# Quantised expert in finer steps: some of VectorE's work on GpSimd and ScalarE, transposes in place of products with ones

## What is computed

```python
x = _layernorm(x + attention(x))        # linear attention, 16 heads, chunks of 128, decay, rotary, RMS norm
x = _layernorm(x + expert(x, fside, ctx))   # one expert per batch entry
x = _layernorm(x + ffn(x))              # fp4 weights, silu gate, I = 1408, RMS of the output

def _smooth_quant_linear(x, w):
    s = max(sqrt(max(amax_x, EPS) / max(amax_w, EPS)), EPS)   # maxima over rows, one per column
    xs, ws = x / s, w * s
    x_scale = max(rowmax|xs|, EPS) / 127;  w_scale = max(rowmax|ws|, EPS) / 127
    x_q = clip(round(xs / x_scale), -127, 127);  w_q = clip(round(ws / w_scale), -127, 127)
    return x_q @ w_q.T * x_scale * w_scale.T

def _expert_forward(xe, guw, dw):       # guw 512x512, dw 512x256, both differ per batch entry
    gate, up = split(_smooth_quant_linear(xe, guw))
    return _smooth_quant_linear(silu(gate) * up, dw)
```

## Time and profile before

| | |
|---|---|
| median of 3 runs | 863.43 us (862.97 to 863.92) |
| the profiled execution, its time | 862.34 us |
| its span | 860.5 us |
| PE, DVE, ACT, POOL busy | 87%, 63%, 37%, 15% |
| mean granted TensorE clock | 0.936 |

### The profile page before, as it was taken

One profiled execution on the slowest core, in us unless ns is written; L12 is line 12 of the kernel. 1 busy time (PEld: TensorE's weight loads), 2 busy tenths in 40 slices (PEclk: granted clock), 3 DMA queues, 4 the chain that ended last, 5 costly groups with the idle time before them and its releaser, 6 DMA issues.

```text
span 860.5 us, 12175 instructions
## 1 busy us (share of the span) xinstructions
PE 749.3 (87%) x4742; PEld 612.8 (71%) x4742; DVE 544.0 (63%) x1032; ACT 321.1 (37%) x559; POOL 129.4 (15%) x173
## 2 busy tenths in 40 slices
PE   4799988887998799525999999999999999899993
PEld 3688777766877587414888777886768877688882
DVE  3567578775667758769771847855578746542214
ACT  4232232225422432157443335353443544341312
POOL 0452334023322233044000000000000000000000
PEclk9899999997998899655999999999999999999997
DMA  8400100013100130040102012002111030010201
GB/s 306 171 26 1 38 13 13 1 26 123 32 7 1 38 99 1 1 147 1 50 1 74 0 50 98 1 25 98 48 53 45 0 122 1 1 50 0 98 1 49
DMA packets 25356, 41.11 MB, mean 48 GB/s; under 512 B 4954, under 2 KB 7642, under 8 KB 25178
## 3 DMA queue, kind: packets, MB, share of 16 engines
q1 hardware_dynamic: 23194, 37.27, 12.9%
q10 hardware_dynamic: 2112, 3.15, 1.1%
HBM read 28.88 MB, written 11.53 MB: 47 GB/s over the span
## 4 chain that ended last, share of the span: by engine, by line
PE 39%; DVE 8%; ACT 2%; issue 2%; DVEq 0%; ACTq 0%
PE ps L1460 24%; PE ps L1470 11%; PE ps L457 2%; DVE act_s L279 2%; PE ps L468 2%; DVE act_s L376 1%; DVE silu L1393 1%; ACT silu L1330 1%; PE ps L477 1%; DVE xc L1406 1%; ACT h_hi L1313 1%; DVE xb L406 1%; DVE e_stats L409 1%; PE ps L450 1%; DVE w L279 0%
## 5 line engine op out<-in xcount | busy, mean ns | idle before, releaser
L1460 PE MATMUL ps<-x2T_lo,wgu_hi 128*128 128x512 f32 x352 | 141.1, 401 | 0.8 <-DVE x2T_lo L1383 0.8
L1460 PE MATMUL ps<-x2T_hi,wgu_lo 128*128 128x512 f32 x352 | 137.3, 390 | 0.0
L1460 PE MATMUL ps<-x2T_hi,wgu_hi 128*128 128x512 f32 x352 | 137.2, 390 | 0.0
L1393 DVE TENSOR_TENSOR silu<-ps,silu 128x512 f32<-128x512 f32 x44 | 30.4, 690 | 100.2 <-PE ps L1460 99.9
L1045 PE MATMUL ps<-wqkv_lo,xT_hi 128*128 128x512 f32 x192 | 83.0, 433 | 10.5 <-DVE masked L972 6.2
L1045 PE MATMUL ps<-wqkv_hi,xT_lo 128*128 128x512 f32 x192 | 78.4, 408 | 0.0
L1045 PE MATMUL ps<-wqkv_hi,xT_hi 128*128 128x512 f32 x192 | 78.2, 407 | 0.0
L1460 PEld LDWEIGHTS ps<-x2T_lo,wgu_hi 128*128 128x128 f32 x352 | 66.2, 188 | 15.3 <-DVE x2T_lo L1383 1.5
L1460 PEld LDWEIGHTS ps<-x2T_hi,wgu_lo 128*128 128x128 f32 x352 | 66.1, 188 | 14.0
L1460 PEld LDWEIGHTS ps<-x2T_hi,wgu_hi 128*128 128x128 f32 x352 | 66.2, 188 | 12.9
L1470 PE MATMUL ps<-wdn_lo,h_hi 128*128 128x512 f32 x176 | 70.6, 401 | 3.7 <-DVE h_lo L1377 3.7
(11 more groups left out here) (170 smaller groups left out, 1473.8 us busy)
## 6 DMA issues: line engine op xcount, KB each, us to landing
x_in<-in_x_dram SPq DMA_DIRECT2D x16, 256.0 KB, 3.5
w<-in_fside_BxS2xS_dram SPq DMA_DIRECT2D x4, 1024.0 KB, 6.5
x_dram<-xb SPq DMA_DIRECT2D x4, 1024.0 KB, 5.1
xc<-x_dram SPq DMA_DIRECT2D x4, 1024.0 KB, 5.4
xb<-x_dram SPq DMA_DIRECT2D x3, 1024.0 KB, 5.4
out_dram<-xc SPq DMA_DIRECT2D x3, 1024.0 KB, 4.2
z<-in_x_dram SPq DMA_DIRECT2D x3, 768.0 KB, 4.7
x_dram<-z SPq DMA_DIRECT2D x3, 768.0 KB, 4.0
```

The lines of the kernel that those rows point to most:

```text
L1393: nc.vector.tensor_tensor(silu[:, it % 2, :], ps[5][:, :], silu[:, it % 2, :], ALU.mult)\
L1460: last = nc.tensor.matmul(dst[:, :], lhs, rhs, start=(k == 0 and n == 0), stop=(k == NK - 1 and n == 2))
```

## The change

What it does:
- The expert's steps get finer names, each with its own place; column maxima of w and x are taken in halves (`w_maxima`, `w_maxima2`, `x_maxima`, `x_maxima2`).
- Clips, gate product and the residual adds go from VectorE to GpSimd (`pool_steps`), which in feed-forward has a block of its own that runs the expert's steps in order. Normalising goes to ScalarE, as a scale and a shift.
- `rows_of` transposes a column that is read with zero stride 128 times, instead of multiplying a diagonal with ones; the diagonals (L306) go.
- In attention the state add goes to GpSimd, the fp8 conversion of decoded words to ScalarE (`scale_values`); `decode` stands ahead of `x_lo`; `ln_root_of` stands behind the two projection drains; ScalarE's place 2 stands ahead of the rms root.
- In the weight stage GpSimd builds all diagonals but five.

The core of the diff:

```diff
-EXPERT_STEPS = {"w_maxima": 0, "x_maxima": 3, "smooth": 5, "scale_x": 7, "scale_w": 9, "clip": 11, "xq01": 13,
...
+EXPERT_STEPS = {"w_maxima": 0, "w_maxima2": 1, "x_maxima": 3, "x_maxima2": 3, "columns": 4, "ratio": 4, "root": 4, "smooth": 5, "rows": 5, "scale_x": 6,
...
+                "silu": 18, "gate": 18, "a_maxima": 19, "columns2": 19, "ratio2": 20, "root2": 20, "smooth2": 20,
...
+                "sum23": 29, "e_root": 29, "shift": 29, "normalise": 30}
...
-EXPERT0_STEPS = {"w_maxima": (4, 2), "x_maxima": (5, 2), "smooth": (6, 0), "scale_x": (6, 2), "scale_w": (7, 2),
...
+EXPERT0_STEPS = {"w_maxima": (1, 2), "w_maxima2": (2, 2), "x_maxima": (4, 2), "x_maxima2": (5, 0), "columns": (5, 0), "ratio": (5, 1), "root": (5, 2),
...
+                 "y01": (15, 0), "rescale_y01": (15, 1), "y23": (15, 1), "add01": (15, 1), "rescale_y23": (15, 1),
...
+        def normalise(b):
+            act.wait_ge(self.x2_shift, b + 1)
+            for c in range(NC):
+                nc.scalar.activation(xb[:, c, :], xb[:, c, :], ACT.Identity, bias=small[:, 14, c:c + 1],
+                                     scale=small[:, 13, c:c + 1]).then_inc(self.x2_done, 1)
...
+            for c in range(0, NC, 2):
+                pool.wait_ge(self.rounded, (b * 4 + 2 * layer + weights) * NC + c + 2)
+                nc.gpsimd.tensor_scalar(src[:, c:c + 2, 0:width], src[:, c:c + 2, 0:width], ROUND + QMAX,
+                                        ROUND - QMAX, ALU.min, ALU.max).then_inc(self.clipped, 1)
...
             for k in range(kt):
-                last = nc.tensor.matmul(self.bank(use)[:, k * P:(k + 1) * P], ones, diag[:, (count + 1) % 2, k, :],
-                                        start=True, stop=True)
+                last = nc.tensor.transpose(self.bank(use)[:, k * P:(k + 1) * P],
+                                           small[:, column, k:k + 1].broadcast_to([P, P]), ident)
...
-                if c == 0 and b > 0:
-                    ln_root_of(b - 1)
                 if n + 1 < CHUNKS:
                     projected(n + 1, 0)
                     projected(n + 1, 1)
+                if c == 0 and b > 0:
+                    ln_root_of(b - 1)
...
+                scale_values(n)
+                beside(steps, n, 2)
                 wait_full(act, "ss", n)
...
-BUILDERS = ("pool", "act", "pool", "pool", "dve")
+BUILDERS = ("pool", "act", "pool", "pool", "pool", "pool", "pool")
```

More of the change, by code:

```diff
@@ L267, in vector_steps @@
-        silu_g, e_var, e_root, x2_done, mom = self.silu_g, self.e_var, self.e_root, self.x2_done, self.mom
+        nc, w, v, xb, act_s = self.nc, self.w, self.v, self.xb, self.act_s
+        scale_row, small, stats, mv = self.scale_row, self.small, self.stats, self.mv
+        left, right = slice(0, HALF), slice(HALF, E)
         linked = 0
@@ L340, in x_maxima @@
-        def x_maxima(b):
+            scale = nc.vector.tensor_scalar(small[:, slot + 1, :], small[:, slot, :], Q_EPS, 1.0 / QMAX, ALU.max, ALU.mult)
+            if use[0] in "wv":
+                scale.then_inc(self.columns_ready, 1)
+                layer = int(use[0] == "v")
+                dve.wait_ge(self.columns_ready, b * 4 + 2 * layer + 2)
+            else:
+                then_wait(b, scale)
+            nc.vector.reciprocal(small[:, slot + 2, :], small[:, slot + 1, :]).then_inc(self.inv_ready, 1)
@@ L341, in x_maxima, with w_maxima @@
+        def w_maxima(b, columns):
+            dve.wait_ge(self.w_in, (b + 1) * 16)
+            column_max(w, columns, act_s[:, 1, :])
+        def x_maxima(b, columns):
             if isinstance(b, int) and b == 0:
-                dve.wait_ge(x1_done, NC)
+                dve.wait_ge(self.x1_done, NC)
             else:
-                dve.wait_ge(x1_in, b * 16)
-            column_max(xb, E, act_s[:, 0, :])
-        def smooth(b):
-            smoothing(b, 0)
-            on_diagonal(0, small[:, 5, :], NK)
-            on_diagonal(1, small[:, 4, :], NK)
@@ L353, in scale_activations @@
[L353 to L368 removed]
+                dve.wait_ge(self.x1_in, b * 16)
@@ L370, in rescale, with a_maxima @@
+            column_max(xb, columns, act_s[:, 0, :])
+        def v_maxima(b):
+            dve.wait_ge(self.v_in, (b + 1) * 16)
+            column_max(v, left, w[:, 0, HALF:E])
+        def a_maxima(b):
+            dve.wait_ge(self.gated, b + 1)
+            column_max(act_s, left, act_s[:, 0, HALF:E])
         def rescale(b, prefix, chunks):
@@ L437, in vector_steps @@
-            "y01": lambda b: residual(b, (0, 1)),
-            "y23": lambda b: residual(b, (2, 3)),
-            "normalise": normalise,
+            "w_maxima": lambda b: w_maxima(b, left),
+            "w_maxima2": lambda b: w_maxima(b, right),
+            "x_maxima": lambda b: x_maxima(b, left),
+            "x_maxima2": lambda b: x_maxima(b, right),
+            "ratio": lambda b: ratio(b, 0),
+            "smooth": lambda b: smooth(b, 0),
+            "scale_x": lambda b: scale_columns(b, "x_rows", xb, E),
@@ L509, in tensor_steps @@
         return {
-            "smooth": columns_first,
-            "scale_x": rows_first,
+            "columns": columns_first,
+            "rows": rows_first,
             "xq01": lambda b: quantised(b, ("xq0", "xq1"), act_s, 0),
@@ L852, in _ @@
         def _(pool):
+            steps = expert.pool_steps(pool)
             def rotate(n):
@@ L876, in _ @@
             for n in range(CHUNKS):
-                c = n % NC
+                b, c = divmod(n, NC)
+                beside(steps, n, 0)
                 if 1 <= c < NC - 1:
@@ L884, in _ @@
                     rotate(n + 1)
+                beside(steps, n, 1)
+                if 1 <= c < NC - 1:
+                    wait_drained(pool, "kv", n)
+                    pool.wait_ge(kv_decayed, b * (NC - 2) + c)
+                    nc.gpsimd.tensor_tensor(kv[:, c % 2], kv[:, c % 2], kv_old[:, :, :], ALU.add).then_inc(kv_done, 1)
                 wait_drained(pool, "attn", n)
@@ L1368, in _, with expert_of @@
             out_root(B - 1)
+        @block.gpsimd
+        def _(pool):
+            steps = expert.pool_steps(pool)
+            def expert_of(b):
+                for name in EXPERT_STEPS:
+                    if name in steps:
+                        steps[name](b)
+            for b in range(1, B):
+                expert_of(b)
         @block.vector
```

297 lines of the change are left out of this document (133 added, 164 removed), and 7 rows, old and new, of tables (EXPERT0_STEPS, EXPERT_STEPS).

## The result

| | before | after |
|---|---|---|
| median of 16 runs each | 863.92 us (861.89 to 864.71) | 865.42 us (863.46 to 866.99) |
| profiled execution, its time | 862.34 us | 866.59 us |
| its span | 860.5 us | 864.8 us |

The ratio is 1.0018, interval 1.0011 to 1.0026: slower by 0.18%, or 1.5 us. The side was the likelier one of the prediction, and the size is 6.6 us smaller than the forecast of 872. By the bound that the prediction set itself, 0.2%, this counts as no change, to which it had given 0.07.

A forecast was written before the change was run, and what follows sets the result against it. TensorE was taken to set the end nearly everywhere. Attention -20.9, weights -1, feed-forward +19.4 and clock +12 summed to +9.5 on 862.3 us, 871.8, given as 872, range 852 to 885.

The forecast's parts named there:

- clock in feed-forward: Feed-forward: the new long waits lower TensorE's granted clock, costing 12 us, bounds 0 and 18.
- new waits 15.0 against some 5.5: Feed-forward batch hosting an expert: TensorE's new waits sum to 15.0 us, against some 5.5 before.
- The two long waits: Feed-forward: TensorE waits for column maxima, 5.7 us at first columns (2.6 in first hosting batch), 4.5 at second columns.
- The first rows: Feed-forward: TensorE waits 1.0 us for the smoothing reciprocal, with columns and a down projection filling 0.87 + 2.73 us.
- The three small ones: Feed-forward: second gate_up products, `aq` behind GpSimd's clip and v_scale wait 0.6 us each, 1.7 together.
- The last down product: Feed-forward: it waits for h_lo, with normalising now ahead of h_hi; between 1.3 and 4.2 us, taken as 2.1.
- it washes out, near 863: Rival for the whole time: attention -23, feed-forward +18, clock +6 us; chance 0.10.
- Chunks 12 to 14: Attention: 65.8 us before; chunk 12 becomes 27.1 with waits for columns, o_hi and rows; a gain of 1.8.
- Chunk 15 and the tail: End of attention: normalising on ScalarE stands ahead of the last rms; 27.8 us becomes 30.8, a loss of 3.0.
- The signs named under "right": Hosting batches: both column waits over 4 us, clock under 1.00, 122 to 127 us; attention: no score product waiting for drains.
- 11.5 us of drain waits: Attention: score products' waits for two ScalarE drains go in full, with the root behind the two projection drains.
- The contention rival: GpSimd beside VectorE: h_lo and integer scaling stretch 0.25 us, clips 2.1, zero-stride loads cost 9.2; 884 us, chance 0.14.

The follow-up runs named there:

- experiment 7: The kernel before with only the 80 products of ones by a diagonal replaced by transposes of a zero-stride column: 853.52 us, ratio 0.9903.
- experiment 6: The version of experiment 4 plus later columns and rows, earlier output steps and reordered ScalarE steps in attention: 817.81 us, ratio 0.9467 to the kernel before.
- experiment 8: Layer norm root behind the projection drains in the kernel before: 858.37 us, ratio 0.9947; that edit undone in the changed kernel: 864.92 us, 1.0014 to the kernel before.
- experiment 5: The changed kernel with only the normalising one place later in the feed-forward: 863.94 us, ratio 1.0010 to the kernel before.
- experiment 3: The changed kernel with both the first and the second column transposes two places later: 844.18 us, ratio 0.9776 to the kernel before.
- experiment 4: The version of experiment 3 plus weights' rounding behind the first two drains and normalising one place later: 828.98 us, ratio 0.9602 to the kernel before.

## Why the prediction was right and wrong

Put beside each other, profiled execution against profiled execution:

| term | predicted | measured |
|---|---|---|
| attention, chunk 1 to its end | -20.9 | -19.9 |
| weights | -1 | -1.1 |
| feed-forward, waits | +26.3 | +19.2 |
| feed-forward, matmuls | -6.9 | -6.9, taken over |
| clock in feed-forward | +12 | +11.2 |
| start-up | 0 | +1.6 |
| the rest | 0 | +0.2 |
| sum | +9.5 | +4.3 |

Measured attention runs from 49.41 to 358.30 us against 47.84 to 376.60. The feed-forward terms come from the windows: idle time (length less TensorE's busy time) of the three hosting batches rose from 14.4 to 33.6 us. Busy time rose by 4.3 us although 60 cheaper transposes took 6.9 away, for which experiment 7 has the price; what is left, 11.2 us, is half clock.

**The step that failed is the sum of the waits in a feed-forward batch**, "new waits 15.0 against some 5.5". In the batch from 514.5 us TensorE is idle 12.2 us against 5.2. The two long waits were right within 0.6 us: 5.1 (predicted 5.7) and 4.1 (4.5), and 2.4 (2.6) in the first batch, with 4.0 (4.5) at the second columns there. The small ones were not. The first rows (1.0) never waited: the two things that were to fill the time, columns and down product, ran at half clock and took 2.0 and 3.8 us, not 0.87 and 2.73. A wait and the slow stretch behind an earlier wait fill the same time, and the prediction charged both. The three small ones came to 0.8, not 1.7. `aq` never waited: GpSimd's clips in that layer are of 512 elements and take 0.61 us, and the last of the first pair ended 0.05 us before its transposes. The last down product waited 1.6, not 2.1. A wait of 0.5 at the split of x2, which the sum lacked, goes the other way. In all 7.1 us too much over three batches. The time came out nearest to the rival "it washes out, near 863" (0.10), but not by its split, which had +6 for the clock.

**What was right.** The clock came to 11.2 against 12, in part by luck. Batch by batch it took 4.8, 3.6 and 2.8 us where 3.2, 5 and 5 were forecast, and the price was read from chunks 7 and 8 without a wait of 2.5 us for o_lo that stands in the same window. The transposes were put at the lower bound, 0.109 us, and experiment 7 shows that on its own. Chunks 5 and 6, 7 and 8, 9 to 11 came to 38.6, 39.9 and 57.3 us against 39.1, 40.5 and 57.3; the weight stage to 31.5 against 31.8. Chunks 12 to 14 took 65.7 against 64.0, of which chunk 12 had 1.2 us: its columns waited less (3.4, not 4.8), o_lo less (1.1, where 2.3 was put on o_hi), its rows more (1.8, not 0.9), and the wait for the rms root (1.1), which the prediction names, had no price in its sum. Chunk 15 and the tail lost 3.6 against 3.0; that the normalising ahead of the last root made this loss is argued, since experiment 6 moved it together with other steps. The signs named under "right" were seen: both column waits over 4 us in the two later hosting batches with the maxima as releaser (in the first the first columns waited 2.4, as its own sum had it), the clock under 1.00, no score product waiting for a drain. Of the batches the first, at 121.1 us, fell just short of the 122 to 127, and the others, at 123.3 and 122.4, lie at its lower end.

The waits of TensorE in attention in the changed kernel (its L448, L476 and L456 are the expert's), beside which the earlier trace rows had 22.6 us in two lines:

```profile
PE ps L1130 <- DVE o_lo L1008: 7.4, 4, 2.8
PE ps L448 <- DVE act_s L317: 4.0, 2, 3.4
PE ps L476 <- DVE act_s L392: 3.3, 1, 3.3
PE ps L456 <- DVE small L344: 3.3, 2, 1.8
```

**What was right in its sum and wrong in its reason.** The prediction gave the 11.5 us of drain waits to the root's move "in full". Experiment 8 shows that this edit alone gains 8.6 us of the whole time in one half of the executions of the kernel before and about 1 in the other, and that undoing it in the changed kernel costs nothing. So the drain waits go when the root is moved, and they go without that where VectorE is relieved and the steps stand finer. Two parts of a change that cure the same wait can't both be credited with it.

**The contention rival** (0.14) fell as a forecast of the time: h_lo took 0.721 us in the mean over 44, against 0.692, so 0.03 more and not 0.25; a clip of 1024 elements took 1.04, not 2.1; the zero-stride loads cost as little as plain ones. But its mechanism is in the traces, and dearer for a single instruction than the rival had it. In the changed kernel the 38 h_lo with no GpSimd work beside them take 0.693 us, and the three with GpSimd busy for over half of their length take 1.11. Few of them meet it, so it comes to 1.2 us in the whole run (31.7 against 30.5). In attention it comes to more. The instruction that joins sign and magnitude of the decoded words has two inputs in SBUF. GpSimd was busy beside it, for over half of its length, in 2 of 16 before and in 15 of 16 now that `decode` stands earlier. Its duration is given in ns as least, median and most, before and then now:

```profile
L910 DVE TENSOR_TENSOR magnitude<-magnitude,sign x16: 707/709/1128, 48.5 to 362.6; 128x1056 uint16<-128x1056 uint16 x16
...
L938 DVE TENSOR_TENSOR magnitude<-magnitude,sign x16: 849/1128/1137, 47.2 to 339.2; 128x1056 uint16<-128x1056 uint16 x16
```

That is 5.6 us more of VectorE's time in the run (17.8 against 12.2). Chunks 1 to 3 took 51.64 us both times, so none of it reached TensorE there; what it costs in later chunks was not tried. The 0.94 us of the earlier trace rows is such a mixture too: four of the eight adds ran alone and took 0.69, the others beside GpSimd took up to 1.57. The masks, with one input in PSUM, take 0.68 us with GpSimd busy beside them or not. The Trainium skill (GPSIMD Engine Reference, the table of the engine), by which GpSimd's SBUF interfaces are shared with VectorE, in contention with VectorE instructions that have two SBUF inputs, agrees with these rows.

**The executions.** Start-up differs by 1.6 us between the two profiles, and this belongs to the executions: experiment 5 has the change's own start-up code, and its shared wait in chunk 3 lies at 91.26 us, that of before at 91.18, that of the change at 92.75. The profile of before lies 1.6 us below its median and that of after 1.2 above. So of the 4.3 us between the profiles 1.5 are left between the medians, and of the forecast's 6.6 us too much 7.1 stand in the waits, 1.0 the other way in attention; the remainder is within what two executions differ by. The wait in chunk 3 lies between 90.8 and 92.9 us in the profiles of all versions.

**What stays open.** The experiments in feed-forward were run with attention as the change has it, and the parts of the work taken off VectorE were not tried one by one, apart from the clips. The two groups of executions in experiment 8 have no cause yet. Why taking the 4.1 us wait away gave back 2.5 us of busy time per batch, and the 5.1 us wait none, was not tried either.

## What to carry to other kernels

Steps cut finer are only as good as their places: in an order shared by engines a supplier has to stand as many places ahead of its consumer as the engines drift apart. Two column steps that stood too early cost this change about the 20 us that attention had won, and experiment 3 got 21 back by moving table entries alone. Don't judge the removal of one wait by that wait alone: the second columns' gave 17 us, the first columns' and the normalising's next to nothing, since the next in line took their time or the half clock stayed. With no wait over 1.4 us left, TensorE's busy time itself was 3.6 us less in the second hosting batch (experiment 4). When adding up predicted waits, put them in one order of time, because the slow stretch behind one wait hides the next.

## What the runs showed of the hardware

- A transpose whose loaded operand is one column of 128 partitions read with stride zero takes 0.109 us, like a plain one (experiment 7), half of the 0.224 us of the fp32 product of ones by a diagonal.
- On GpSimd a clip (one input, two constants) of 128x1024 f32 takes 1.04 us and of 128x512 0.61, while adding two 128x512 inputs takes 1.28 and multiplying two 128x1024 ones 2.36. The second input more than doubles the price of these. The Trainium skill (GPSIMD Engine Reference, section 3.1) gives about 2.6 cycles per element for two inputs and 1.03 where the ports are the bound, for an engine of 1.2 GHz. An estimate from these rates alone is 2.22 and 0.88 us for 1024 elements, and 1.11 and 0.44 for 512; the trace has 0.14 to 0.17 us more each time, so it agrees with the rates and adds a fixed part. The prediction took its 1.7 us for the clip between bounds from a two-input row, which is why it was too dear. VectorE took 0.65 to 0.69 for the same clip and 0.69 for the same add.
- A VectorE instruction with two inputs in SBUF takes longer while GpSimd is busy: 0.69 us becomes 1.11 (h_lo, 128x512 f32), and 0.71 becomes 1.13 (128x1056 uint16). With one input in PSUM (the masks) it stays at 0.68.
- The conversion of 1056 f16 values to fp8 with a scale takes ScalarE 2.09 us, against 1.16 on VectorE before, reading them in an interleaved order. In chunks 1 to 3 it cost no time: they took 51.64 us with ScalarE busy for 21.28 us, as with 14.15 before.

The main groups by line and shape of the changed kernel that these numbers come from, with count, busy us and mean ns:

```profile
L806 ACT ACTIVATE shared<-magnitude 128x1056 fp8e4<-128x1056 f16 x16 | 33.4, 2086 | 12.9 <-DVE magnitude L938 12.9
L1393 DVE TENSOR_TENSOR h_lo<-silu,h_hi 128x512 fp32r<-128x512 f32 x44 | 31.7, 721 | 45.7 <-ACT h_hi L1317 45.7
...
L290 POOL TENSOR_TENSOR xb<-xb,act_s 128x512 f32<-128x512 f32 x16 | 20.2, 1281 | 41.9 <-DVE act_s L392 41.9
...
L284 POOL TENSOR_TENSOR act_s<-act_s 128x1024 f32<-128x1024 f32 x4 | 9.5, 2364 | 81.3 <-ACT act_s L237 81.3
...
L279 POOL TENSOR_SCALAR act_s<-act_s 128x1024 f32<-128x1024 f32 x8 | 8.4, 1044 | 134.5 <-ACT act_s L217 134.4
```
